# Reordering the hand-over from attention to the experts: expert sums ahead of the routers, two routers between the first pair's tiles

## The chip, the cores and the metric

One core of a Trainium2 chip runs the whole program. The metric is the device time of one execution in microseconds (us), as the median over several runs. TensorE is called PE, VectorE DVE, ScalarE ACT, GpSimd POOL and SyncE SP. Each engine works through its own queue of instructions in order; semaphores tie the queues together.

## The reference, cut to what matters

There are B = 4 batches of 512 tokens with D = 512 features. A cross-attention block of smoothed int8 products comes first, then a feed-forward block with 8 experts of which the two with the largest summed logits are used for all tokens:

```python
x = x + _L0_xattn_ref(_layernorm(x), fside_BxS2xS2_0, ctx_1024)

# _L0_ffn_ref(_layernorm(x), ...)
x = hidden_states.reshape(-1, d)                      # 2048 tokens x 512
router_logits = x @ gate_w.T                          # 2048 x 8
_, sel = jax.lax.top_k(router_logits.sum(axis=0), 2)  # two experts for all tokens
rw = jax.nn.softmax(router_logits[:, sel], axis=1)
w1s, b1s, w2s, b2s = w1[sel], b1[sel], w2[sel], b2[sel]
h = jax.nn.gelu(jnp.einsum('nd,kdf->knf', x, w1s) + b1s[:, None, :])
y = jnp.einsum('knf,kfd->knd', h, w2s) + b2s[:, None, :]
out = jnp.einsum('nk,knd->nd', rw, y)                 # added to x
```

## The kernel before

The first part (to about 131 us of the span) is the quantised attention block: four batches, two products each, with transposes on PE between them. Its PSUM is handed out as four "slots" of two banks; `SLOT_USES` lists by hand who uses each slot in which order, `fill` waits until the earlier uses of a slot are drained, and `drained` counts them.

The second part is the feed-forward block. The 16 "pairs" (2 experts x 8 strips of 256 hidden features) each multiply all 2048 tokens, in two halves (tp = 0, 1), with the strip's up-projection, apply GELU and multiply with the down-projection. The 15 later pairs use Strassen's scheme with seven products instead of eight; the first pair is computed plainly (`plain`, line 850) while the operands of Strassen's scheme are still being made. All products are fp32 in two parts: each operand is split into a rounded "hi" part (ACT casts) and a remainder "lo" part (subtraction on DVE or POOL), and hi*hi, hi*lo and lo*hi are accumulated. A plain tile is 12 products of 128x512.

The hand-over between the two parts is where the diff lies. For each batch b and feature half h:

- `normed2(b, h)` on PE (line 656) transposes the normalised tokens into slot use `y.b.h`.
- ACT copies them to SBUF (`keep_full`, line 961, which also sums over tokens, or `keep_summed`, line 968, where DVE's `token_sums`, line 1334, makes the sum), then rounds them (`keep_hi`, line 973). DVE makes the remainder (`keep_lo`, line 1291), the "split".
- `router(b)` on PE (line 667): 8 products that give the logits of all 512 tokens of a batch; ACT's `keep_logits` (line 982) copies them to SBUF. `logit_columns(b)` (line 685) transposes them into bank 3, and DVE's `pick_logits` (lines 1361 to 1368) takes the two chosen experts' columns; POOL raises e to their difference (`pow`, line 523), DVE makes the softmax weights (`token_weights`, lines 1519 to 1523). Every later `outputs_of` (line 1541), which adds a weighted product of the down-projection to the residual and frees the PSUM bank for PE, needs these weights.
- `token_total` (line 1342) adds the token sums, `expert_sums` on PE (line 677) multiplies them with the gate's weights, `choose_experts` on DVE (lines 1346 to 1349) finds the two experts; SP waits for that, reads the numbers and loads the first strip of weights, `raw1` (line 285) and `raw2` (line 289). ACT's `first_weights` (line 985) rounds the four blocks of `raw1`, DVE's (line 1381) makes the remainders; then the first plain tile can start.
- POOL's `inv_std(b, 2)` (lines 340, 341: a `pow` and a product) gives the second normalisation's factors; batch 3 is normalised half by ACT (line 895) and half by DVE (`normalise_last`, line 1323).

The order in each queue is written out by hand. Before, on PE: `normed2(3, 1)`, `router(1)`, `expert_sums`, `router(0)`, `router(2)`, `router(3)`, then in the first pair tiles 0 and 1, the logit columns, tiles 2 and 3, the four `down` groups (line 805: 48 products for two token groups of 512 and two feature strips), then the second half likewise. On DVE the `keep_lo` of all batches stand ahead of the remainders of the first weights. The second half of `down` starts a bank only after `outputs_of` has freed it (`y_free`).

## Time and profile before

| | |
|---|---|
| median of 3 runs | 820.45 us (818.23 to 821.61) |
| span of the profiled execution | 818.7 us |
| PE busy | 771.5 us (94%) |
| DVE / ACT / POOL busy | 477.7 / 354.6 / 449.7 us |
| mean granted clock of PE | 0.979 of full speed |
| chain that ended last | PE 83%, POOL 8%, DVE 3% |

Of the profiled execution only the span, from the first to the last instruction, is shown; it lies 1.75 us under the median of the runs and inside their spread. The views are read as follows. A timeline line gives start, duration (of a merged run of instructions, from the first's start to the last's end), engine, line of the kernel, operation, destination and source, shape, and how many; square brackets give the idle time of the engine ahead of it and who ended it. PE's ends are modelled, so successive products overlap in the record: their pitch is read from starts. The granted clock is a share of 2.4 GHz, so 0.50 is the level of 1.2 GHz.

### The profile page before, as it was taken

To read this page: it belongs to the slowest core of one execution; us is meant where nothing else is said; L and a number is where in the kernel's file an instruction comes from. 1 tells how busy PE (TensorE), PEld (TensorE's weight loads), DVE (VectorE), ACT (ScalarE), POOL (GpSimd) and SP (SyncE) were. 2 spreads that over 40 slices of the span, in tenths; PEclk is the share of its full clock that TensorE was granted. 3 is DMA by queue.
4 is the path that set the end of the run, shared out by engine and by line. 5 is a ranking of instruction groups with operands and counts; after the bars stand their busy time and mean duration, and the time that the engine had idled before them with its cause. 6 is when DMAs were issued, how large, how long until landed. Compare 5 with 4: busy or idle time off the path is not lost.

```text
span 818.7 us, 11342 instructions
## 1 busy us (share of the span) xinstructions
PE 771.5 (94%) x3570; PEld 624.1 (76%) x3577; DVE 477.7 (58%) x669; ACT 354.6 (43%) x660; POOL 449.7 (55%) x497
## 2 busy tenths in 40 slices
PE   5688666999999999999999999999999999999998
PEld 4666455688788888888888888888888888888886
DVE  5999759797754545454545454545454545454545
ACT  3967588743442434343424343434343434242422
POOL 1789997157564646464646464646464646464622
PEclk9899968999999999999999999999999999999999
DMA  9400000301010101010101010101010101010022
GB/s 344 173 2 1 1 0 2 129 1 51 1 52 1 51 0 49 3 50 2 48 4 51 1 45 6 42 9 44 7 41 11 36 15 36 15 32 19 0 103 104
DMA packets 19077, 32.34 MB, mean 39 GB/s; under 512 B 872, under 2 KB 11240, under 8 KB 18160
## 3 DMA queue, kind: packets, MB, share of 16 engines
q1 hardware_dynamic: 18896, 31.98, 11.1%
q8 instruction: 12, 0.20, 0.1%
q10 hardware_dynamic: 160, 0.08, 0.0%
q14 instruction: 9, 0.07, 0.0%
HBM read 27.87 MB, written 4.19 MB: 39 GB/s over the span
## 4 chain that ended last, share of the span: by engine, by line
PE 83%; POOL 8%; DVE 3%; issue 2%; ACT 2%; DMA 1%; ACTq 0%; POOLq 0%; DVEq 0%
PE slot L805 42%; PE slot L792 34%; PE slot L850 3%; POOL wv L366 2%; POOL xf L383 1%; PE slot L667 1%; POOL wv L372 1%; POOL cv L366 1%; PE slot L585 1%; DVE rmax L1226 1%; DMA b_rows<-in_L_ffn_b 1%; POOL rstd L340 1%; POOL h_lo L476 1%; DVE stats L1217 1%; DVE peak_x L1226 1%
## 5 line engine op out<-in xcount | busy, mean ns | idle before, releaser
L792 PE MATMUL slot<-xo,a_hi 128*128 128x512 f32 x840 | 259.1, 390 | 0.0
L1541 DVE SCALAR_TENSOR_TENSOR res<-slot,rw,res 128x512 f32<-128x512 f32 x256 | 178.5, 750 | 130.3 <-PE slot L805 130.2
L1570 DVE TENSOR_TENSOR e<-slot,e 128x512 f32<-128x512 f32 x150 | 103.8, 692 | 173.4 <-PE slot L792 173.3
L805 PE MATMUL slot<-w_hi,h_hi 128*128 128x512 f32 x512 | 201.3, 393 | 0.4 <-POOL h_lo L476 0.4
L805 PE MATMUL slot<-w_lo,h_hi 128*128 128x512 f32 x512 | 199.6, 390 | 0.0
L805 PE MATMUL slot<-w_hi,h_lo 128*128 128x512 f32 x512 | 199.4, 390 | 0.0
L792 PEld LDWEIGHTS slot<-xo,a_hi 128*128 128x128 f32 x840 | 157.4, 188 | 33.3 <-DVE e L1570 0.2
L476 POOL TENSOR_TENSOR h_lo<-e,h_hi 128x512 fp32r<-128x512 f32 x96 | 138.1, 1451 | 55.0 <-ACT e L1104 54.0
L792 PE MATMUL slot<-xo,a_lo 128*128 128x512 f32 x420 | 163.7, 390 | 0.0
L805 PEld LDWEIGHTS slot<-w_hi,h_hi 128*128 128x128 f32 x512 | 96.1, 188 | 25.1 <-POOL h_lo L476 5.6
L476 POOL TENSOR_TENSOR h_lo<-hid,h_hi 128x512 fp32r<-128x512 f32 x32 | 44.1, 1378 | 124.7 <-ACT hid L1104 124.7
L805 PEld LDWEIGHTS slot<-w_hi,h_lo 128*128 128x128 f32 x512 | 96.2, 188 | 20.1
L805 PEld LDWEIGHTS slot<-w_lo,h_hi 128*128 128x128 f32 x512 | 96.2, 188 | 19.3
L792 PEld LDWEIGHTS slot<-xo,a_lo 128*128 128x128 f32 x420 | 78.9, 188 | 16.5
L1103 ACT ACTIVATE h_hi<-e,b_now 128x512 fp32r<-128x512 f32 x90 | 64.9, 721 | 58.0 <-DVE e L1570 57.6
L1142 ACT COPY e<-slot 128x512 f32<-128x512 f32 x30 | 17.6, 587 | 164.5 <-PE slot L792 164.5
L490 POOL TENSOR_TENSOR a_lo<-raw,a_hi 128x256 fp32r<-128x256 f32 x45 | 34.3, 761 | 95.9 <-ACT a_hi L988 95.9
L991 ACT CAST w_hi<-raw 128x512 fp32r<-128x512 f32 x32 | 19.8, 622 | 109.8 <-PE slot L805 109.8
L495 POOL TENSOR_TENSOR w_lo<-raw,w_hi 128x512 fp32r<-128x512 f32 x30 | 38.7, 1289 | 50.4 <-ACT w_hi L991 50.4
L1104 ACT ACTIVATE e<-e,b_now 128x512 f32<-128x512 f32 x90 | 63.8, 709 | 0.0
L1103 ACT ACTIVATE h_hi<-slot,b_now 128x512 fp32r<-128x512 f32 x38 | 26.2, 689 | 66.5 <-PE slot L792 56.6
L490 POOL TENSOR_TENSOR a_lo<-ssum,a_hi 128x256 fp32r<-128x256 f32 x60 | 43.7, 739 | 0.0
(145 smaller groups left out, 814.5 us busy)
## 6 DMA issues: line engine op xcount, KB each, us to landing
raw<-in_L_ffn_w SPq DMA_DIRECT2D x32, 512.0 KB, 3.4
res<-in_x SPq DMA_DIRECT2D x4, 1024.0 KB, 11.9
wv<-in_fside_BxS2xS SPq DMA_DIRECT2D x4, 1024.0 KB, 12.8
out_x<-res SPq DMA_DIRECT2D x3, 1024.0 KB, 3.9
cv<-in_ctx SPq DMA_DIRECT2D x4, 512.0 KB, 13.1
out_x<-res SPq DMA_DIRECT2D x4, 256.0 KB, 2.7
b_row<-in_L_ffn_b SPq DMA_DIRECT2D x2, 256.0 KB, 4.6
b_rows<-in_L_ffn_b ACTq DMA_DIRECT2D x1, 64.0 KB, 6.0
```

The costliest lines, as they stand in the source:

```text
L366: g.tensor_tensor(w[:, j, :], w[:, j, :], rows[b][:, 0:n], ALU.mult).then_inc(wmul_ready[b], 1)
L476: g.tensor_tensor(h_lo[:, i, :], hid[i][:, :], h_hi[:, i, :].bitcast(F32), ALU.subtract).then_inc(h_ready, 1)
L490: g.tensor_tensor(a_lo[:, i, :, :], A_OF[i], a_hi[:, i, :, :].bitcast(F32), ALU.subtract).then_inc(a_ops_ready, 1)
L495: g.tensor_tensor(w2_lo[:, f, :], raw2[:, f, :], w2_hi[:, f, :].bitcast(F32), ALU.subtract).then_inc(w2_ready, 1)
L792: last = t.matmul(dst, a[:, i, k, :], xo[tp][:, v, k, :], start=(start and n == 0), stop=(n == 3 * H - 1), skip_group_check=True)
L805: last = t.matmul(y_bank[j][:, :], a[:, i, j * P:(j + 1) * P], v[:, f, :], start=(start and n == 0), stop=(not start and n == 2), skip_gro ...
L850: last = t.matmul(TILE_BANK[n], a[:, 2 * f + h, k, :], xo[q][:, v, k, :], start=(m == 0), stop=(m == 3 * KD - 1))
L991: s.copy(w2_hi[:, f, :], raw2[:, f, :]).then_inc(w2_hi_ready, 1)
L1103: s.activation(h_hi[:, i, :], src, ACT.Gelu_apprx_tanh, bias=bias).then_inc(hid_ready, 1)
L1104: s.activation(hid[i][:, :], src, ACT.Gelu_apprx_tanh, bias=bias).then_inc(hid_ready, 1)
L1541: v.scalar_tensor_tensor(out=r, in0=y_bank[j][:, :], scalar=rw[:, ds(p, 1), n:n + 1].rearrange("p a b -> p (a b)"), in1=r, op0=ALU.mult, o ...
L1570: v.tensor_tensor(dst[:, :], src, other[:, :], ALU.add).then_inc(comb_ready, 1)
```

## The change

- PE: `expert_sums` moves ahead of all routers; of these only `router(1)` and `router(0)` stay ahead of the first plain tile, `router(2)` goes behind tile 0 and `router(3)` behind tile 1; the logit columns go from behind tile 1 to behind tile 2. 28 transposes of the identity into a spare bank (`keep_clock`) are added ahead of `normed2(2, 0)` and 12 ahead of `normed2(3, 0)`.
- PE: in a plain tile the products go hi*hi, hi*lo, lo*hi by groups of two; the wait ahead of them is for the rounded weights alone, and the wait for the weights' remainders stands ahead of lo*hi.
- DVE: `normalise_last` is first behind `moments(3, 2)`; `keep_lo(0, 0)` and `keep_lo(0, 1)` go behind `choose_experts`; then come `pick_experts`, `pick_bias`, `first_weights`, and only then the splits of batches 2 and 3, then the first down weights. `last_operands(0)` and `fourth_operand(0)` go ahead of `pick_logits`.
- ACT: `keep_summed(3, 1)` moves ahead of the roundings of batch 2, `keep_logits(1)` between those of batches 2 and 3, `keep_logits(0)` behind the first weights, `keep_logits(2)` and the first down weights behind the GELUs of tile 0, `keep_logits(3)` behind those of tile 1.
- SP: the first load of `raw1` is split in two of half its size, each with a semaphore of its own.
- The slots of the four routers' results are dealt out anew. POOL's order is unchanged.

```diff
@@ SLOT_USES
-             "r.0 "),
+             "r.1 "),
...
-             "a.2 s2.0 p2.0.1 y.3.1 r.3 "),
+             "a.2 s2.0 p2.0.1 y.3.1 "),
...
-             "s2.2 p2.1.1 p2.2.1 wq2.3 p2.3.0 y.1.1 y.2.0 r.1 "),
+             "s2.2 p2.1.1 p2.2.1 wq2.3 p2.3.0 y.1.1 y.2.0 r.0 "),
...
-             "p1.2.0 r2.0 wq1.3.0 r2.1 xq2.0 a.3 wq2.1 wq2.2 p2.2.0 s2.3 p2.3.1 y.1.0 y.2.1 e r.2 "),
+             "p1.2.0 r2.0 wq1.3.0 r2.1 xq2.0 a.3 wq2.1 wq2.2 p2.2.0 s2.3 p2.3.1 y.1.0 y.2.1 e r.2 r.3 "),
@@ SP
-            load_w1(0)
+            first = w1_v[ds(expert[0], 1), 0].rearrange("e p k f -> (e p) k f")
+            sp.dma_start(raw1[:, 0:H, :], first[:, 0:H, :]).then_inc(raw1_top, 16)
+            sp.dma_start(raw1[:, H:KD, :], first[:, H:KD, :]).then_inc(raw1_load, 16)
@@ PE
+            def keep_clock(n):
+                i, uses = place("y.3.1")
+                pe.wait_ge(drained[i], uses)
+                for _ in range(n):
+                    t.transpose(slot[i][:, 1, 0:P], ident[:, :], ident[:, :])
...
             normed2(1, 1)
+            keep_clock(28)
             normed2(2, 0)
             normed2(2, 1)
+            keep_clock(12)
             normed2(3, 0)
             normed2(3, 1)
+            expert_sums()
             router(1)
-            expert_sums()
             router(0)
-            router(2)
-            router(3)
@@ plain
-                        pe.wait_ge(a_ops_ready, 2 * f + h + 1)
+                        pe.wait_ge(a_hi_ready, 2 * f + h + 1)
                     pe.wait_ge(lo_ready[b], h + 1)
                     hi, lo = HI_AT[s][h], LO_AT[s][h]
-                    for k in range(H):
-                        for a, v in ((a_hi, hi), (a_hi, lo), (a_lo, hi)):
+                    for a, v in ((a_hi, hi), (a_hi, lo), (a_lo, hi)):
+                        if q == 0 and a is a_lo:
+                            pe.wait_ge(a_ops_ready, 2 * f + h + 1)
+                        for k in range(H):
@@ PE, first pair
+            up_tile(0, 0)
+            router(2)
+            up_tile(0, 1)
+            router(3)
+            up_tile(0, 2)
+            logit_columns(0)
+            logit_columns(1)
+            logit_columns(2)
+            logit_columns(3)
+            up_tile(0, 3)
+            first_downs(0)
@@ ACT
+            keep_summed(3, 1)
             keep_hi(2, 0)
             keep_hi(2, 1)
-            keep_summed(3, 1)
+            keep_logits(1)
             keep_hi(3, 0)
             keep_hi(3, 1)
-            keep_logits(0)
-            keep_logits(1)
             first_weights(0, 2)
             first_weights(2, 4)
             s.activation(gelu_warm[:, :], half[:, 0:1], ACT.Gelu_apprx_tanh)
-            keep_logits(2)
-            keep_logits(3)
-            first_down_weights()
+            keep_logits(0)
...
+            first_bias()
+            gelu_tile(0, 0)
+            keep_logits(2)
+            first_down_weights()
+            gelu_tile(0, 1)
+            keep_logits(3)
+            gelu_tile(0, 2)
+            gelu_tile(0, 3)
@@ DVE
             moments(3, 2)
-            keep_lo(0, 0)
+            normalise_last()
             keep_lo(1, 0)
-            normalise_last()
             token_sums(2)
-            keep_lo(1, 1)
             token_sums(3)
             token_total()
+            keep_lo(1, 1)
+            choose_experts()
+            keep_lo(0, 0)
             keep_lo(0, 1)
-            choose_experts()
+            pick_experts()
+            pick_bias()
+            first_weights(0, 2)
+            first_weights(2, 4)
             keep_lo(2, 0)
             keep_lo(2, 1)
             keep_lo(3, 0)
             keep_lo(3, 1)
-            first_weights(0, 2)
-            first_weights(2, 4)
-            pick_experts()
-            pick_bias()
-            first_down_weights()
-            pick_logits()
...
+            first_down_weights()
+            last_operands(0)
+            fourth_operand(0)
+            pick_logits()
+            token_weights()
+            outputs_of(0, 0, 0)
```

## Rows read from the trace of the kernel before

**Rows 1.** The page of the profile: the span.
```profile
span 818.7 us, 11342 instructions
```

**Rows 2.** The chain that ended last, in order of time: start, length, piece.
```profile
153.71 5.47 PE slot L850 x24
...
165.97 10.88 PE slot L805 x48
```

**Rows 3.** PE's timeline through the hand-over.
```profile
122.37 1.04 PE L616 MATMUL slot<-ident,cv 128*128 128x128 f32 x8
...
134.49 0.41 PE L656 MATMUL slot<-ident,xf 128*128 128x128 f32 x2 [3.44 <-POOL xf L396]
...
139.89 3.87 PE L656 MATMUL slot<-ident,xf 128*128 128x128 f32 x16 [0.81 <-ACT xf L895]
...
146.38 0.95 PE L677 MATMUL slot<-gwt_full,tok_total 128*128 128x8 f32 x8
147.19 6.52 PE L667 MATMUL slot<-xo,gwt 128*16 128x512 f32 x24
...
159.11 1.17 PE L685 MATMUL slot<-ident,logits 16*128 16x16 f32 x16
...
165.81 0.39 PE L805 MATMUL slot<-w_hi,h_hi 128*128 128x512 f32 x1
```

**Rows 4.** Busy time by stretch: length; PE, PEld, DVE, ACT, POOL; clock; DMA share, GB/s.
```profile
83.00:84.00 1.00, 0.00 (x0) 0.06 (x2) 0.82 (x1) 0.72 (x1) 0.95 (x2) 1.00 0.00 0
...
135.00:136.00 1.00, 0.55 (x3) 0.30 (x4) 0.93 (x8) 1.00 (x3) 1.00 (x3) 0.72 0.00 0
...
145.00:146.00 1.00, 1.00 (x5) 0.31 (x3) 0.87 (x3) 1.00 (x2) 0.00 (x0) 0.66 0.00 0
```

**Rows 5.** DVE's timeline through the hand-over.
```profile
135.98 2.86 DVE L1291 TENSOR_TENSOR xo<-xf,xo 128x1024 fp32r<-128x1024 f32 x2
...
143.79 1.23 DVE L1334 TENSOR_REDUCE tok_sum<-slot 128x2 f32<-128x1024 f32 x1 [1.59 <-PE slot L656]
145.15 0.17 DVE L1342 TENSOR_REDUCE tok_total<-tok_sum 128x4 f32<-128x16 f32 x1
...
147.38 0.17 DVE L1346 COPY sum_row<-slot 128x8 f32<-128x8 f32 x1 [0.93 <-PE slot L677]
...
147.94 4.61 DVE L1291 TENSOR_TENSOR xo<-xf,xo 128x1024 fp32r<-128x1024 f32 x4
152.60 1.43 DVE L1381 TENSOR_TENSOR a_lo<-raw,a_hi 128x256 fp32r<-128x256 f32 x4
...
155.84 0.29 DVE L1375 TENSOR_REDUCE b_col<-picked 128x16 f32<-128x128 f32 x1
...
162.44 0.18 DVE L1366 TENSOR_TENSOR lsub<-lmin,lmax 128x16 f32<-128x16 f32 x1
...
166.60 1.24 DVE L1519 TENSOR_TENSOR lexp<-lpow,is_top 128x16 f32<-128x16 f32 x2
...
170.07 2.73 DVE L1541 SCALAR_TENSOR_TENSOR res<-slot,rw,res 128x512 f32<-128x512 f32 x4
```

**Rows 6.** ACT's timeline: rounding of batch 2, and of the first weights.
```profile
144.13 2.01 ACT L973 CAST xo<-xf 128x1024 fp32r<-128x1024 f32 x2
...
152.16 1.33 ACT L985 CAST a_hi<-raw 128x256 fp32r<-128x256 f32 x4 [1.87 <-DMA raw<-in_L_ffn_w]
```

**Rows 7.** POOL's timeline: the powers, and the remainders of the hidden tiles.
```profile
34.58 1.03 POOL L340 TENSOR_TENSOR rstd<-var_e,neg_half 128x4 f32<-128x4 f32 x1
...
136.60 1.97 POOL L340 TENSOR_TENSOR rstd<-var_e,neg_half 128x4 f32<-128x4 f32 x1
...
162.69 2.90 POOL L523 TENSOR_TENSOR lpow<-euler,lsub 128x16 f32<-128x16 f32 x1 [0.84 <-DVE lsub L1366]
165.56 3.43 POOL L476 TENSOR_TENSOR h_lo<-e,h_hi 128x512 fp32r<-128x512 f32 x2
```

**Rows 8.** SP's timeline: the issue of the first weights.
```profile
148.99 0.39 SPq L285 DMA_DIRECT2D raw<-in_L_ffn_w  x1
```

More of the change, by code:

```diff
@@ L881, in _, with first_downs @@
-            first_pair()
+                if n == 3:
+                    pe.wait_ge(hid_ready, 8 + 8 * tp + 2)
+                if tp == 0 and n == 0:
+                    pe.wait_ge(drained[0], ALL_DRAINED[0])
+                if tp == 0 and n == 2:
+                    pe.wait_ge(drained[1], ALL_DRAINED[1])
+                plain(tp, n)
+            def first_downs(tp):
+                if tp == 0:
+                    pe.wait_ge(w2_ready, 2)
+                    pe.wait_ge(drained[2], ALL_DRAINED[2])
+                    pe.wait_ge(drained[3], ALL_DRAINED[3])
+                down(0, tp, 0, 0, 0, True)
+                down(0, tp, 0, 1, 1, False)
+                last = down(0, tp, 1, 2, 1, True)
+                if tp == 1:
+                    last.then_inc(w2_free, 1)
+                down(0, tp, 1, 3, 0, False)
@@ L882, in _ @@
+            up_tile(0, 0)
[9 more added lines that the diff above has]
+            first_downs(0)
+            for n in range(4):
+                up_tile(1, n)
+            first_downs(1)
+            pe.wait_ge(hid_ready, 8 + 16)
             pair(1, True, False)
@@ L1173, in pair @@
                         down_hi(0)
-            first_pair()
+            first_bias()
[6 more added lines that the diff above has]
+            gelu_tile(0, 3)
+            operand_hi(0, (T2H, T2L), 4)
+            operand_hi(0, (T3H, T3L), 4)
+            operand_hi(0, (T1H, T1L), 4)
+            operand_hi(0, (T4H, T4L), 4)
+            for n in range(4):
+                gelu_tile(1, n)
+            later_weights()
             pair(1, True, False)
@@ L1596, in pair @@
                         operand_lo(1, 3)
-            first_pair()
+            first_down_weights()
[4 more added lines that the diff above has]
+            outputs_of(0, 0, 0)
+            middle_operands(0, 3)
+            middle_operands(0, 4)
+            outputs_of(0, 0, 1)
+            operand_lo(0, 0)
+            operand_lo(0, 1)
+            operand_lo(0, 2)
+            operand_lo(0, 3)
+            last_operands(1)
+            fourth_operand(1)
+            dve.wait_ge(b2_load, 16 * TOPK)
+            bias_rows(0)
+            outputs(0, 1)
             pair(1, True, False)
```

91 lines of the change are left out of this document (28 added, 63 removed).

## The prediction

> **What bounds the kernel now.** I read the page first: a span of 818.7 us [rows 1]. The chain that ended last, in order of time, is then PE alone from the first plain tile on [rows 2]: 24 products of line 850 are followed by 48 of line 805 without a gap, and so on to the end, so whatever comes ahead of that stretch or opens a gap in it is added to the total one for one, and work of other engines inside it costs nothing while PE isn't kept waiting. Therefore the timelines of the hand-over decide, PE's first [rows 3]: idle for 3.44 us up to 134.49; 16 transposes of batch 3 from 139.89 in 3.87 us, where 8 elsewhere take 1.04; then router 1, the expert sums at 146.38, three routers from 147.19, the first plain tile (it begins behind them, 153.55), the logit columns at 159.11, the first down product at 165.81. The stretches say why batch 3's transposes are slow [rows 4]: the granted clock fell from 2.4 to 1.2 GHz inside 135 to 136, after PE's idle time, and came back inside 145 to 146. DVE, ACT, POOL and SP then show what the first tile waits for [rows 5 to 8]. The point that I compare is the start of the first down product, 165.81 before: all of PE's work ahead of it is the same set in both kernels apart from `keep_clock`, and everything behind it is the same.
>
> **Prices.** A product of 128x512 at full clock has a pitch of 5.47/24 = 0.228 us [rows 2], so a plain tile is 2.73, a router without waits 8 x 0.228 = 1.82, the four down groups 10.88, two of them 5.44. A split on DVE is 1.15 (four in 4.61 [rows 5]), four weight remainders 1.43, `pick_experts` with `pick_bias` 156.13 - 154.03 = 2.1 [rows 5].
>
> **Step 1, up to batch 3's transposes.** 28 transposes at 1.04/8 = 0.13 each at most are 3.6 us; from the end of `normed2(1, 1)` (131.0) they fill the idle 3.44 us and end at 134.3 to 134.7, so they cost at most 0.2 us of a wait that is followed by another wait for POOL. The 12 take 1.4 and end at about 139.4. The clock should stay at 2.4 GHz: in the rows PE is only slowed after such a gap. On DVE the two splits that began at 135.98 leave the time in which POOL computes the last power. That power took 1.97 us beside them and 1.03 otherwise [rows 7], and ACT's and DVE's normalisation of batch 3 hang on it. I take the gain of 0.95: its factors are ready at 137.9 instead of 138.9. PE then transposes from about 139.3 (behind the 12) with 16 x 0.12, and ends at 141.3 instead of 143.76. What the row shows is a power stretched by 0.94 us when DVE's subtractions of two SBUF operands ran beside it. The Trainium skill, "SBUF — State Buffer", section "Who interferes with whom", says that a DVE instruction with two SBUF inputs contends with a GpSimd instruction that reads SBUF, the later one being blocked. By that rule the gain is real; without it the power would stay at 1.97 and the step would be 1 us poorer. The trace agrees with it here.
>
> **Step 2, the choice of experts.** Before: last token sum 143.79 (waiting for PE), total at 145.15, expert sums at 146.38 behind router 1, result read at 147.38, index found at 148.02 [rows 3, 5]. After: `normalise_last`, one split and `token_sums(2)` end at 141.3, `token_sums(3)` 1.2 later, the total at 142.9; PE is free and starts at once, 143.15, the copy at 144.15, the index at 144.8. So 3.2 us earlier, 148.0 to 144.8. SP issued 0.97 after the index [rows 8]; now 145.8. The rounding of the weights began 3.17 after the issue [rows 6], 148.9 for the whole; the first half should be there at about 148.2 (half of 512 KB moves in 0.7 us at the rate of that load, 330 GB/s). ACT is the later one: four roundings at 1.0 [rows 6] from 143.6, with `keep_logits(1)` between them waiting for router 1 (146.0), end at 148.5. First rounded block at 148.9.
>
> **Step 3, PE to the first down product.** Router 1 144.05 to 145.9; router 0 waits for its splits, which now stand behind the choice, and ends at 148.15; PE idles to 148.95. Tile 0 starts there, 4.6 us earlier than 153.55; its remainders are made from 149.35 on and don't hold it. But routers 2 and 3, 3.64 us, now lie behind. Router 2 also waits: DVE goes from 144.8 through two splits (2.3), picking (2.1 and gaps), remainders (1.43, from 149.35) and two splits (2.3) to 153.15, so router 2 ends at 154.1 where PE alone would allow 153.5: 0.55 lost. Then tile 1 156.85, router 3 158.65 (its slot is free once ACT has copied router 2's at 154.7), tile 2 161.4, columns 162.55 (1.15 by [rows 3]), tile 3, first down product at 165.3. Sum: -4.6 + 3.64 + 0.55 = -0.4; by the clock times -0.5. The earlier weights are spent on the routers moved behind them.
>
> **Step 4, the tokens' weights.** Before, the columns were done at 160.3, DVE's difference at 162.62, POOL's power to 165.6, the weights at 170.03, the first output freed its bank at 170.8, and PE's third down group, 5.44 behind the first, wanted it at 171.25: only 0.45 us of slack [rows 3, 5, 7]. After, the columns are 2.3 us later (162.55) though the down products start 0.5 earlier. Picking takes 2.3: difference at 164.9. The power, at 16 columns, is 2.9 by its row. Since it is 1.03 at 4 columns alone, it grows with the columns, and I don't expect it to be shorter with DVE idle: 167.8 (bounds: 1.03, were it all contention, and 2.9). DVE has `last_operands` and `fourth_operand` behind it now, so it starts at once, where it started 1.0 after the power before. Its small operations took 3.4 us there, next to two remainders on POOL (3.43 for two) [rows 5, 7]. The GELUs of tile 2 have been done since 162.7 and those of tile 3 at 166.6, and both remainders stand queued on POOL behind the power, so the same meeting takes place: I take 3.6, with a floor of 1.4 if DVE gets in first (the sum of these operations at their shortest, an estimate). Weights at 171.4, first output done at 172.2 (0.75). PE wants it at 165.3 + 5.44 = 170.75: a stall of 1.4, between 0 and 1.6. By the same section of the Trainium skill the one that comes later waits for the whole instruction, and POOL and DVE are released by the same event. The rule alone leaves either order open, which is my floor and my ceiling.
>
> **Step 5, behind it.** What DVE does in the first pair moves back by 1.4 as PE does: middle operands to 176.7, outputs to 179.5, remainders 184, last operands 189.7, bias 193.1. PE wants the second half's first bank at 177.6 + 10.92 + 5.44 = 194.0, and gets it at 193.8. So nothing is added, up to 0.5 if one of them is stretched. The new semaphore waits of the tiles are met long before.
>
> **Sum.** -0.5 + 1.4 = +0.9 us on the profiled execution, 819.6. The runs' median is 1.75 above the span, so I forecast 820.45 + 0.9 = 821.3. The measurement tells about 0.5%, 4.1 us, from no change.
>
> **Rivals.**
> 1. The weights' chain doesn't hold PE up: DVE's small operations get in ahead of POOL's remainders. Against it stand the 3.4 us of the same operations before. Then only -0.5 is left: 820.0, with somewhat more if a split or the picking ends sooner. Chance 0.27.
> 2. Slower: the clock. In the new order PE idles from 141.3 to 143.1 for the token sums, then 0.3 and 0.8 us within 147 to 149. If the clock drops to 1.2 GHz as it did in 135 to 136, each product of 128x512 costs twice, and the rows' low stretch lasted 10 us under broken work. Five microseconds of low clock on work that isn't waiting cost 2.5, ten cost 5, added to +0.9: 823.8 to 826.2. For it: the fall at 135 followed idle time. Against: PE had nothing to do for all of 83 to 84 at a clock of 1.00 [rows 4]. [...] Chance 0.12. The Trainium skill, "TensorE: Matmul & The Clock Gate", section "What's actually happening", says that the clock depends on how busy the array has been recently and that throttled is the default; it names no price for gaps like these.
> 3. The change doesn't do what it says: `keep_clock` doesn't keep the clock, or POOL's power stays long. Batch 3's transposes then end 1 to 2 us later and the whole chain with them: +1.9 to +2.9, 822.3 to 823.4. Chance 0.15.
> 4. The front gains more than I have worked out, because PE's order has more freedom: the most is what PE's own work allows. From 139.3 it has 1.9 + 0.95 + 4 x 1.82 + 4 x 2.73 + 1.15 = 22.2 us, so the down products can't start before 161.5, 4.3 us earlier. That needs all waits of steps 2 to 4 to vanish. A gain of 1 to 3 us: chance 0.05.
>
> The forecast itself has 0.41. **Range**: 818.0 to 824.5; it takes in rivals 1 and 3 and the milder end of 2, and the 1.7 us by which the runs scatter. Faster by over 0.5% would need rival 4 whole: 0.03. Slower by over 0.5% is the hard end of rival 2, or 2 with 3: 0.07. Within: 0.90.
>
> **What would show it.** Clock 1.00 from 131 to the end; the power of batch 3 at 1.03; the index at 144.8; first tile at 149, with a gap of under 1 us ahead of it; router 2 waiting for DVE's split; first down product at 165.3; then a gap of 1.4 in PE at about 170.8, ended by DVE's line 1541 behind the weights. If the gap is missing, step 4 is wrong; if the clock shows 0.50 behind 141, rival 2 it is; if the first down product comes before 164 or after 167, steps 2 and 3 are.

## The result and the profile after

| | before | after |
|---|---|---|
| median | 819.89 us (818.23 to 821.80, 7 runs) | 822.36 us (821.68 to 823.69, 7 runs) |
| span of the profiled execution | 818.7 us | 820.3 us |
| mean granted clock of PE | 0.979 | 0.985 |
| ratio to before, with its 95% interval | | 1.0039 [1.0024, 1.0053] |

The forecast was 821.3 us, within 818.0 to 824.5, with a change of under half a per cent as the likeliest outcome. That is what came: the change makes the kernel a little slower. By the two medians the loss is 2.5 us (a quotient of 1.0030); the ratio of 1.0039 on record, with its interval, puts it at 2.0 to 4.3 us. Between the two profiled executions it is 1.6 us; I had +0.9.

The page of the profile after, its span and its first part (busy time, share, instructions):

```profile
span 820.3 us, 11435 instructions
PE 773.2 (94%) x3617; PEld 624.6 (76%) x3617; DVE 479.4 (58%) x669; ACT 354.7 (43%) x660; POOL 448.7 (55%) x497
```

PE is busy 1.7 us longer than before: the 40 transposes of `keep_clock` add 4.7 (3.22 and 1.47), and at the full clock batch 3's transposes and router 1 take less. PE's timeline of after, through the hand-over, to be read against [rows 3]:

```profile
130.58 3.22 PE L666 MATMUL slot<-ident 128*128 128x128 f32 x28
...
138.86 2.10 PE L659 MATMUL slot<-ident,xf 128*128 128x128 f32 x16
142.58 1.06 PE L686 MATMUL slot<-gwt_full,tok_total 128*128 128x8 f32 x8 [1.62 <-DVE tok_total L1377]
143.49 4.23 PE L676 MATMUL slot<-xo,gwt 128*16 128x512 f32 x16
148.57 1.17 PE L862 MATMUL slot<-xo,a_hi 128*128 128x512 f32 x4 [0.85 <-ACT a_hi L1008]
...
152.12 2.16 PE L676 MATMUL slot<-xo,gwt 128*16 128x512 f32 x8 [0.57 <-DVE xo L1326]
...
161.52 1.16 PE L695 MATMUL slot<-ident,logits 16*128 16x16 f32 x16
...
165.49 0.39 PE L815 MATMUL slot<-w_hi,h_hi 128*128 128x512 f32 x1
...
170.71 0.39 PE L815 MATMUL slot<-w_hi,h_lo 128*128 128x512 f32 x1
172.57 0.47 PE L815 MATMUL slot<-w_hi,h_hi 128*128 128x512 f32 x1 [1.48 <-DVE res L1574]
```

Everything that the change says is there: the 16 transposes of batch 3 take 2.10 us instead of 3.87, the expert sums start at 142.58 instead of 146.38, the first plain tile at 148.57 instead of 153.55. And yet the first down product starts at 165.49 instead of 165.81. Behind it is what before didn't have: PE stands still at the third down group, for 172.57 - 170.71 - 0.23 = 1.63 us, until DVE has written the first output. From the first down product's start to the end nothing else is new: the only further gap in the groups of this line is 0.4 us for a POOL remainder, as in before.

DVE's timeline of after, against [rows 5]:

```profile
142.36 0.17 DVE L1377 TENSOR_REDUCE tok_total<-tok_sum 128x4 f32<-128x16 f32 x1
...
144.16 0.16 DVE L1384 FIND_INDEX8 top_i<-top_v,sum_row 128x8 uint32<-128x8 f32 x1
...
150.76 5.73 DVE L1326 TENSOR_TENSOR xo<-xf,xo 128x1024 fp32r<-128x1024 f32 x4
...
164.91 0.17 DVE L1401 TENSOR_TENSOR lsub<-lmin,lmax 128x16 f32<-128x16 f32 x1
...
168.17 1.27 DVE L1552 TENSOR_TENSOR lexp<-lpow,is_top 128x16 f32<-128x16 f32 x2 [2.91 <-POOL lpow L524]
169.36 1.27 DVE L1553 TENSOR_SCALAR lden<-lpow 128x16 f32<-128x16 f32 x1
170.66 0.25 DVE L1554 RECIPROCAL lrec<-lden 128x16 f32<-128x16 f32 x1
170.95 0.69 DVE L1556 TENSOR_TENSOR rw<-lexp,lrec 128x128 f32<-128x128 f32 x2
```

POOL's of after, against [rows 7]; then ACT's (the rounding of the first block and of the other three) against [rows 6], and SP's issue against [rows 8]:

```profile
136.32 1.00 POOL L343 TENSOR_TENSOR rstd<-var_e,neg_half 128x4 f32<-128x4 f32 x1
...
165.17 2.90 POOL L524 TENSOR_TENSOR lpow<-euler,lsub 128x16 f32<-128x16 f32 x1 [5.19 <-DVE lsub L1401]
168.03 2.56 POOL L479 TENSOR_TENSOR h_lo<-e,h_hi 128x512 fp32r<-128x512 f32 x2
```

```profile
147.92 0.40 ACT L1008 CAST a_hi<-raw 128x256 fp32r<-128x256 f32 x1
149.29 1.02 ACT L1008 CAST a_hi<-raw 128x256 fp32r<-128x256 f32 x3 [0.97 <-DMA raw<-in_L_ffn_w]
```

```profile
145.29 0.39 SPq L294 DMA_DIRECT2D raw<-in_L_ffn_w  x1
```

The end of the chain that ended last, before and then after (start, length, piece): it is 1.52 us later.

```profile
803.73 9.02 PE slot L805 x39
```

```profile
805.25 9.03 PE slot L815 x39
```

### The profile page after: what moved, and what is told of

Its sections match the earlier page's. It is cut to its first block, busy times and chain, and to the rows that moved or that the text cites. A ratio compares the mean times of both kernels' runs of the same rounds, so it can differ in the third digit from the quotient of the medians.

```text
span 820.3 us, 11435 instructions
## 1 busy us (share of the span) xinstructions
PE 773.2 (94%) x3617; PEld 624.6 (76%) x3617; DVE 479.4 (58%) x669; ACT 354.7 (43%) x660; POOL 448.7 (55%) x497
## 4 chain that ended last, share of the span: by engine, by line
PE 80%; POOL 8%; DVE 5%; issue 3%; ACT 2%; DMA 1%; SPq 0%; ACTq 0%; POOLq 0%; DVEq 0%
PE slot L815 41%; PE slot L802 34%; PE slot L862 2%; POOL wv L369 2%; POOL xf L386 1%; POOL wv L375 1%; POOL cv L369 1%; PE slot L588 1%; DVE rmax L1261 1%; DMA b_rows<-in_L_ffn_b 1%; POOL h_lo L479 1%; DVE stats L1252 1%; DVE peak_x L1261 1%; PE slot L638 1%; ACT xf L918 1%
## 5 line engine op out<-in xcount | busy, mean ns | idle before, releaser
L1163 ACT COPY e<-slot 128x512 f32<-128x512 f32 x30 | 17.6, 587 | 164.4 <-PE slot L802 164.4
```

What stands on the lines that cost most here:

```text
L1163: s.copy(e1[:, :], x_bank).then_inc(e1_ready, 1)
```

## The experiments

Executions differ ahead of the part in question: the start of POOL's last normalising (`xf<-res,rstd,nmr`), which I call N, lies at 133.0 to 134.6 us in kernels whose code is the same up to there but for the first transposes of `keep_clock`. So I compare distances: "front" is the start of the first down product minus N, "rest" is the span minus N. The ratios are those on record, with their intervals; they are not exactly the quotients of the medians shown (the two differ by up to 0.0009, most in after), so a difference of less than 0.1% between kernels is not told by either. Each profile is one execution.

| kernel | N | normalising / power on POOL | front | rest | median (runs) | ratio |
|---|---|---|---|---|---|---|
| before | 133.58 | 3.05 / 1.97 | 32.23 | 685.1 | 819.89 (7) | |
| after | 133.30 | 3.05 / 1.00 | 32.19 | 687.0 | 822.36 (7) | 1.0039 [1.0024, 1.0053] |
| e1_clock_alone | 134.43 | 4.05 / 1.96 | 30.90 | 684.1 | 820.51 (12) | 1.0003 [0.9991, 1.0016] |
| e2_no_clock | 133.81 | 3.05 / 1.00 | 32.71 | 687.3 | 823.27 (5) | 1.0041 [1.0028, 1.0054] |
| e3_hid2_first | 133.82 | 3.01 / 1.01 | 33.41 | 688.4 | 823.1 (5) | 1.0035 [1.0022, 1.0048] |
| e4_front_alone | 133.25 | 3.05 / 1.00 | 31.05 | 684.2 | 819.5 (11) | 0.9997 [0.9988, 1.0005] |
| e5_one_load | 134.47 | 3.01 / 1.01 | 32.15 | 687.0 | 822.69 (12) | 1.0032 [1.0021, 1.0043] |
| e6_pool_waits | 134.63 | 3.05 / 1.00 | 32.29 | 685.3 | 821.09 (12) | 1.0013 [1.0003, 1.0024] |
| e7_both | 133.60 | 3.01 / 1.01 | 32.07 | 685.2 | 820.69 (12) | 1.0011 [1.0, 1.0022] |
| e8_pool_split | 133.74 | 3.05 / 1.00 | 29.94 | 683.1 | 818.8 (12) | 0.9983 [0.9972, 0.9995] |
| e9_before_again | 133.72 | 4.09 / 1.97 | 33.31 | 686.6 | 820.05 (10) | 0.9997 [0.9983, 1.0011] |
| e10_router_in_gap | 134.53 | 3.05 / 1.01 | 31.24 | 684.3 | 819.5 (12) | 0.999 [0.9978, 1.0002] |
| e11_before_third | 134.44 | 3.05 / 1.97 | 29.99 | 682.9 | 819.17 (1) | |
| e12_split_no_clock | 133.00 | 3.05 / 1.00 | 32.24 | 685.1 | 820.6 (12) | 1.0008 [0.9997, 1.0019] |

Rest less front is what the kernel takes from the first down product to its end. It is 654.6 to 655.0 us in the four kernels whose profile has the stall at the third down group (after, e2, e3, e5), and 652.9 to 653.3 in the ten others: 1.8 us apart in the mean, with nothing between.

### e1_clock_alone: before, with only `keep_clock`

```diff
             normed2(1, 1)
+            keep_clock(28)
             normed2(2, 0)
             normed2(2, 1)
+            keep_clock(12)
             normed2(3, 0)
```

> The kernel before with the 28 and 12 transposes of keep_clock and nothing else. Theory (batch 3's transposes at 1.2 GHz delay the expert sums, and only DVE's splits stand between these and tile 0): the last transpose ends at about 142.2 instead of 143.8, router 1 fits into PE's wait for the token sums, the index is found at 145.7 instead of 148.0, the four splits follow, tile 0 starts near 151.3 instead of 153.55, and since the routers stay ahead of tile 0 and the columns behind tile 1, no stall appears in the down products: 2.2 us faster than before, ratio 0.997. Rival (the clock is worth nothing, since PE waits for DVE and ACT anyway): 1.000, with 40 useless transposes.

The clock stayed at 1.00 through the whole stretch. The front came 1.33 us nearer to N than in before's profile, less than the 2 us that I gave the clock, because POOL's last normalising took 4.05 us instead of 3.05: DVE's splits had caught it. By medians the gain isn't there at all: 1.0003. The profile and the medians contradict each other here, and this is where the study turned to before itself (e9, e11).

### e2_no_clock: after, without `keep_clock`

```diff
             normed2(1, 1)
-            keep_clock(28)
             normed2(2, 0)
             normed2(2, 1)
-            keep_clock(12)
             normed2(3, 0)
```

> The changed kernel without keep_clock. Theory: the clock falls at about 135, batch 3's transposes end 1.8 later and everything up to the first down product shifts with them, the stall for the tokens' weights stays at 1.6: 1.9 us slower than the changed kernel, 3.4 slower than before, ratio to before 1.004 to 1.006. Rival (the 40 transposes themselves cost time in the changed kernel): equal to the changed kernel or faster.

The clock was 0.50 from 136 to 139.4 and was back before PE had to wait for the token sums; the ratio is after's (1.0041 against 1.0039). So in this order `keep_clock` buys nothing that these runs can tell, since PE has to wait for DVE's token sums anyway. The stall is of the same size, and it has the same releaser:

```profile
173.60 0.47 PE L813 MATMUL slot<-w_hi,h_hi 128*128 128x512 f32 x1 [1.48 <-DVE res L1572]
```

### e3_hid2_first: after, with one of POOL's two remainders ahead of the power

The step in question is Step 4: are the tokens' weights late because POOL's remainders run beside them?

```diff
             hid_lo(0, 0, 1)
-            token_power()
             hid_lo(0, 0, 2)
+            token_power()
             hid_lo(0, 0, 3)
```

> The changed kernel with POOL's remainder of tile 2 ahead of the power. Theory (the stall ahead of the third down group is the tokens' weights, and 2.4 of their 3.5 us is DVE blocked by two remainders on POOL): the remainder is made at about 163 while POOL idles, only tile 3's is left to meet DVE, the weights come 1.2 earlier and the stall falls from 1.6 to about 0.4: 1.2 us faster than the changed kernel, ratio to before about 1.001. Rival (the DVE operations are slow by themselves or wait for something else): the stall stays at 1.6 and the time is that of the changed kernel.

The stall stayed: 174.40 - 172.44 - 0.23 = 1.73 us. POOL's queue behind the power is the reason; its timeline:

```profile
169.77 1.29 POOL L479 TENSOR_TENSOR h_lo<-e,h_hi 128x512 fp32r<-128x512 f32 x1
171.01 0.76 POOL L484 TENSOR_TENSOR ssum<-raw 128x256 f32<-128x256 f32 x1
171.85 0.73 POOL L486 TENSOR_TENSOR ssum<-ssum,raw 128x256 f32<-128x256 f32 x1
```

and DVE's, beside it:

```profile
169.91 1.27 DVE L1552 TENSOR_TENSOR lexp<-lpow,is_top 128x16 f32<-128x16 f32 x2 [2.91 <-POOL lpow L524]
171.09 0.71 DVE L1553 TENSOR_SCALAR lden<-lpow 128x16 f32<-128x16 f32 x1
171.84 0.25 DVE L1554 RECIPROCAL lrec<-lden 128x16 f32<-128x16 f32 x1
172.13 1.34 DVE L1556 TENSOR_TENSOR rw<-lexp,lrec 128x128 f32<-128x128 f32 x2
```

`lexp` ends where the remainder does, `lden` where the first sum of weights does, `rw` only behind the second and third. I had moved one of POOL's instructions away, and the next in its queue took its place; the weights still took 3.56 us. Moving work about in a queue that never runs dry takes no collision away. This run's front is also 1.2 us longer than after's: the second half of the split load landed 5.3 us behind the first issue here, instead of 4.0.

### e6_pool_waits: POOL held back until the weights are made

```diff
             hid_lo(0, 0, 1)
-            token_power()
             hid_lo(0, 0, 2)
+            token_power()
+            pool.wait_ge(rw_made, 1)
             hid_lo(0, 0, 3)
...
             token_weights()
+            dve.sem_inc(rw_made, 1)
             outputs_of(0, 0, 0)
```

> The changed kernel with POOL's remainder of tile 2 ahead of the power and POOL kept idle from the power until DVE has the tokens' weights. Theory (these DVE operations are slow only beside POOL's, whichever they are): they take 1.4 instead of 3.5 us, the first output's bank is free before PE wants it, the stall of 1.5 at the third down group is gone: 1.5 us faster than the changed kernel, ratio to before about 1.002. Rival (the operations are slow by themselves): the stall stays.

DVE's timeline and then POOL's:

```profile
169.60 0.26 DVE L1554 TENSOR_TENSOR lexp<-lpow,is_top 128x16 f32<-128x16 f32 x2 [2.91 <-POOL lpow L525]
169.78 0.17 DVE L1555 TENSOR_SCALAR lden<-lpow 128x16 f32<-128x16 f32 x1
169.98 0.25 DVE L1556 RECIPROCAL lrec<-lden 128x16 f32<-128x16 f32 x1
170.27 0.50 DVE L1558 TENSOR_TENSOR rw<-lexp,lrec 128x128 f32<-128x128 f32 x2
```

```profile
170.90 1.30 POOL L480 TENSOR_TENSOR h_lo<-e,h_hi 128x512 fp32r<-128x512 f32 x1 [1.40 <-DVEq L1622]
```

The same operations take 170.77 - 169.60 = 1.17 us instead of 3.47, PE has no gap at the third down group any more, and the rest falls by 1.7 us while the front is after's. From e3, which has the stall, this kernel differs by the wait alone. This shows what Step 4 said: the stall is POOL's remainders beside DVE's small operations. Its price is 1.8 us by the profiles (from the first down product on), 1.3 by the medians of after and e6, and 2.0 by those of e5 and e7 below, which were measured together, 12 times each, and differ only in this: the larger part of the loss. The power itself stays at 2.90 with nothing beside it.

The rule that I had weighed, in the Trainium skill, "SBUF — State Buffer", section "Who interferes with whom", is that the order of issue decides who blocks. The traces agree where the starts lie clearly apart: in after and in e3 POOL's remainder began 0.14 us ahead of DVE's first operation, and DVE's 0.17 us operations lasted as long as POOL's. It works the other way round too: later in e6, two of POOL's sums of weights of 0.73 us took 1.72 beside DVE's operands. Where the starts are about 0.1 us apart or less they don't tell who waits: in e9 and e1 below, POOL's piece began 0.08 and 0.10 us ahead of DVE's split and was yet the one that waited.

### e5_one_load and e7_both: the first strip loaded in one piece

e5 is after with the diff below; e7 is e6 with it.

```diff
-            sp.dma_start(raw1[:, 0:H, :], first[:, 0:H, :]).then_inc(raw1_top, 16)
-            sp.dma_start(raw1[:, H:KD, :], first[:, H:KD, :]).then_inc(raw1_load, 16)
+            load_w1(0)
...
                     if i == 0:
-                        act.wait_ge(raw1_top, 16)
-                    if i == 1:
                         act.wait_ge(raw1_load, 16)
```

> The changed kernel with the first weights in one load instead of two halves. Theory (the second half lands late: ACT got it 4.0, 4.5 and 5.3 us after the first issue in three profiles of kernels with two halves, the whole load 3.2 and 3.5 after the issue in two with one): the rounding of all four blocks begins 3.2 to 3.5 after the issue, DVE's splits of batch 2 start 0.5 to 1.3 earlier than with the halves, and the down products with them: 0.5 to 1.3 us faster than the changed kernel, ratio to before 1.002 to 1.003. Rival (the late second half is hidden behind PE's own work, or the first half is worth as much): the time of the changed kernel, 1.004.

> Both at once: one load, and POOL idle for the tokens' weights. Theory: the two add up, 2.0 to 2.8 us faster than the changed kernel, which is within 0.5 us of before, ratio 0.9995 to 1.001: what is left of the change is worth nothing, because the moved routers take back what the earlier choice gives. Rival (another part costs too): over 1.002.

In one piece the load is there 3.38 us behind its issue in e5 and 3.46 in e7 (3.17 in before). In two pieces, the first half is used at most 2.63 us behind the first issue (145.29 to 147.92 in after), and the second only 4.00 (after), 4.11 (e6), 4.54 (e2) or 5.30 (e3) behind it. The halves are issued 0.57 apart. Against 3.4 for the whole, that is nearly all of the delay in after and e6, but half or less of it in e2 and e3; why the second half is later still there isn't shown. The first tile then starts earlier, but the remainders of the last weights later, and with them the splits that router 2 waits for: the front is 32.15 and 32.07 against 32.19 and 32.29. The ratios (1.0032 against 1.0039, 1.0011 against 1.0013) don't tell them apart. Splitting the load brings nothing here that these runs can tell.

### e4_front_alone: only the part ahead of the choice of experts

Before with `keep_clock`, the expert sums first, DVE's `normalise_last` first and its splits behind the choice, ACT's `keep_summed(3, 1)` early. The routers and the logit columns stay where before has them.

```diff
+            keep_clock(28)
...
+            keep_clock(12)
...
-            router(1)
             expert_sums()
+            router(1)
...
-            keep_lo(0, 0)
-            keep_lo(1, 0)
             normalise_last()
+            keep_lo(1, 0)
             token_sums(2)
-            keep_lo(1, 1)
             token_sums(3)
             token_total()
-            keep_lo(0, 1)
+            keep_lo(1, 1)
             choose_experts()
+            keep_lo(0, 0)
+            keep_lo(0, 1)
```

> The changed kernel's front (keep_clock, normalise_last first, expert sums ahead of router 1, splits of batch 0 behind the choice) with the routers, columns and splits of batches 2 and 3 where they stood before. Theory: index at 144.5, the six splits end at 151.2, PE runs four routers and starts tile 0 at 152.0, where before started at 153.5; no stall for the tokens' weights, since the columns are behind tile 1: 1.3 us faster than before, 0.9985, and 2.8 faster than the changed kernel, so that the moved routers cost all that and more. Rival (moving the routers helps, and the stall would be there in any case once the front is earlier): slower than before or equal to it.

The front is 31.05, 1.14 nearer than after's, with the same choice of experts (index at N + 10.86 in both). So what after has beyond e4 (two routers behind the tiles, the splits behind the weights, the split load, the order of the products) costs 1.1 us ahead of the first down product, and its late columns cost the stall. Against before's medians e4 gains nothing that can be told (0.9997). Its DVE row says why:

```profile
144.19 6.88 DVE L1299 TENSOR_TENSOR xo<-xf,xo 128x1024 fp32r<-128x1024 f32 x6
```

Six splits behind the choice instead of four (4.61 in [rows 5]). Before makes two of them while POOL computes its power, which costs POOL 0.97 us; here the power is 1.00, but DVE owes 2.3 us of splits later, and the weights, which ACT had begun to round at 148.70, wait for DVE until 150.99.

### e8_pool_split: e4, with one of these splits on POOL

POOL is idle from the last power on. It makes the first split of batch 0, once DVE is through the first of batch 1, so beside token sums that read PSUM and not two operands from SBUF.

```diff
             inv_std(3, 2)
+            pool.wait_ge(hi_ready[0], 1)
+            pool.wait_ge(lo_ready[1], 1)
+            g.tensor_tensor(whole(0, LO_AT[0][0]), part(0, FULL_AT[0][0]),
+                            whole(0, HI_AT[0][0]).bitcast(F32), ALU.subtract).then_inc(lo_ready[0], 1)
...
             choose_experts()
-            keep_lo(0, 0)
+            dve.wait_ge(lo_ready[0], 1)
             keep_lo(0, 1)
```

> e4 with batch 0's first split on POOL, which waits for batch 1's first split and so runs beside the two token sums. Theory (in e4 tile 0 waits for DVE's chain of splits, which runs without a break from the sums to the weights' remainders): one split less on it, tile 0 starts 1.15 earlier than in e4, 1.2 us faster than e4, ratio to before 0.998. Rival (POOL's split takes more from DVE than it gives, or PE's routers are the bound by themselves): that of e4, 0.9997, or worse.

POOL's row, DVE's and PE's:

```profile
140.36 2.36 POOL L473 TENSOR_TENSOR xo<-xf,xo 128x1024 fp32r<-128x1024 f32 x1 [2.32 <-DVE xo L1303]
```

```profile
144.68 5.75 DVE L1303 TENSOR_TENSOR xo<-xf,xo 128x1024 fp32r<-128x1024 f32 x5
```

```profile
143.94 7.65 PE L677 MATMUL slot<-xo,gwt 128*16 128x512 f32 x32
...
163.68 0.39 PE L817 MATMUL slot<-w_hi,h_hi 128*128 128x512 f32 x1
```

The front is 29.94, 1.1 less than e4's, one split of DVE; the four routers run almost without a gap (7.65 us, of which 7.28 are their own work), and the last of them still waits for DVE's last split. With 0.9983 [0.9972, 0.9995] it is faster than both kernels: 0.17% below before, and by the two ratios to before (0.9983 and 1.0039) 0.56% below after (by the medians 0.13% and 0.43%). How much of the gain on before is the order and how much the clock, the next section bears on.

### e9_before_again and e11_before_third: before, profiled again

No edit. The question is how far one profiled execution of before stands for it.

> The kernel before, unchanged, for a second profile. In the profiles so far the span behind the start of POOL's normalisation of batch 2 is 685.1 (before), 687.0 (changed kernel), 685.2 (one load and POOL waiting), while the medians of these differ by 2.5 and 0.9. Theory (what the traces show behind that point is the change's whole cost, and the rest is the time ahead of it, where the code is the same and executions scatter by over 1 us): the second profile of before has 685.1 again behind that point, and its time ahead of it is not 133.6 but nearer to 132.8; ratio 1.000. Rival (the first profile of before was unusual behind that point): it shows 684.4 or less there.

> The kernel before once more, for a third profile. Over 91 executions of this kernel so far the span goes with the mean granted clock: 817.2 to 817.5 us at 0.982 and above, 819.3 and more at 0.979 and below; the two profiles so far are of the second kind (0.979 with 818.7, 0.976 with 820.3), with PE at 1.2 GHz for some 10 us of the hand-over. Theory (the kernel before is two-sided: how long the clock stays low behind PE's idle time, and whether POOL's last normalising is caught behind DVE's split, differ from execution to execution): an execution with a clock of 0.982 or more shows a low stretch of 3.4 to 7 us there, a first down product 31 us behind the start of POOL's normalisation of batch 2 instead of 32.2 or 33.3, and a span near 817.5. Rival (the difference lies elsewhere): 32.2 whatever the clock.

e9, POOL's timeline and then DVE's:

```profile
133.72 4.09 POOL L396 TENSOR_SCALAR xf<-res,rstd,nmr 128x512 f32<-128x512 f32 x4
137.78 1.97 POOL L340 TENSOR_TENSOR rstd<-var_e,neg_half 128x4 f32<-128x4 f32 x1
```

```profile
136.03 2.85 DVE L1291 TENSOR_TENSOR xo<-xf,xo 128x1024 fp32r<-128x1024 f32 x2
```

e11, the stretches (as in [rows 4]), and PE's row:

```profile
136.00:137.00 1.00, 0.67 (x3) 0.43 (x4) 0.93 (x8) 1.00 (x2) 1.00 (x2) 0.80 0.00 0
...
139.00:140.00 1.00, 0.94 (x5) 0.54 (x3) 0.91 (x2) 0.21 (x1) 0.68 (x2) 0.50 0.00 0
140.00:141.00 1.00, 0.25 (x2) 0.21 (x2) 1.00 (x3) 1.00 (x2) 0.00 (x0) 1.00 0.03 8
```

```profile
164.43 0.39 PE L805 MATMUL slot<-w_hi,h_hi 128*128 128x512 f32 x1
```

The same program has fronts of 32.23, 33.31 and 29.99. Two things differ. The normalising is four pieces of 0.77 us, and in before's order the splits begin at almost the same moment as the fourth of them: 0.15 us behind it in before's profile and 0.12 in e11, where the piece took 0.8 and the split 1.7 instead of 1.2, and 0.08 in e9 and 0.10 in e1, where the piece took 1.8 to 1.9 and the split 1.2. A few hundredths of a microsecond go with who waits: half a microsecond for DVE, or one for POOL, on which batch 3 hangs. And the low clock lasted 10 us in before's profile (135.4 to 145.7) and in e9 (136.0 to 146.2), but under 4 in e11 (136.6 to 140), where batch 3's transposes and router 1 found the full clock again. With e1 the four fronts are consistent with a sum: e9 less before is 1.1 and e1 less e11 is 0.9, the caught normalising; before less e11 is 2.2 and e9 less e1 is 2.4, the long stretch of low clock. Over the 95 timed executions of before that were made beside e1 to e12, the mean clock and the span go together: 48 with a clock of 0.982 or more have a median span of 817.4 us, 30 with 0.979 or less one of 819.8, and 17 between them 818.2. That the long stretch is what sets the lower clock of those 30 is worked out from three profiles, not seen in each. By its clock of 0.979 the profile that I predicted from is of the kind of the 30, though its span of 818.7 is among their shortest.

This explains only a part of e1. If the long stretch belongs to a third of before's executions, `keep_clock` has little to remove in the others, and hardly moves a median. But all 12 timed executions of e1 have a clock of 0.982 or more, and still their median span is 818.6 us, 1.2 above that of the 48 of before with such a clock. e4 has `keep_clock` too, but no split beside the normalising, and has 817.6. The caught normalising, 1 us in e1's profile, would account for the difference; whether e1's other executions have it isn't shown. By the same measure e8, with 816.9, is 0.5 us ahead of the 48, and its front of 29.94 is e11's: about half of what it gains on before's median span (817.9) may be the long stretch that it doesn't have.

### e12_split_no_clock: e8 without `keep_clock`

The diff is e2's, on e8.

> e8, the fastest so far, without keep_clock. Theory (a shorter low stretch costs nothing while PE waits for the token sums anyway, as in e2, a longer one up to 2 us): 0.3 to 1 us slower than e8, ratio to before 0.9985 to 0.9995. Rival (the clock is worth nothing behind the new order): 0.9983.

A stretch of e12, its expert sums and its routers, and last the expert sums of e2:

```profile
144.00:145.00 1.00, 1.00 (x5) 0.37 (x5) 0.91 (x6) 1.00 (x2) 0.00 (x0) 0.52 0.00 0
```

```profile
143.09 1.06 PE L687 MATMUL slot<-gwt_full,tok_total 128*128 128x8 f32 x8 [1.62 <-DVE tok_total L1352]
144.01 9.13 PE L677 MATMUL slot<-xo,gwt 128*16 128x512 f32 x32
```

```profile
143.09 1.06 PE L686 MATMUL slot<-gwt_full,tok_total 128*128 128x8 f32 x8 [1.62 <-DVE tok_total L1375]
```

The clock was low from 133.8 to 140.6, came back, and was low a second time from 144.0 to 147.4, behind the 1.6 us in which PE waits for the token sums. The routers took 9.13 us instead of 7.65, and the front is 32.24 instead of 29.94. Of these 2.3 us the first low stretch has 0.8 (the index comes at N + 11.67 instead of 10.86, since PE's slow transposes hold up the token sums) and the second 1.5. By the ratios it is 1.0008 against 0.9983, 2 us, and 1.8 by the medians, where I had expected 0.3 to 1. It is my rival 2, in an order like after's but without `keep_clock`: with the idle time filled ahead of it, the same wait for the token sums left the clock at 1.00 (after, e4 to e8). But the missing transposes alone don't bring it about: e2 lacks them as well, has the same wait of 1.62 us, and kept 1.00 behind it. Its first low stretch was 3.4 us long and e12's 6.8; the cause of the difference isn't shown.

### e10_router_in_gap: can that wait be used?

e8, with router 1 ahead of the expert sums, both of batch 1's splits ahead of the token sums, and after's order of products in a plain tile.

```diff
-            pool.wait_ge(lo_ready[1], 1)
+            pool.wait_ge(lo_ready[1], 2)
...
             normed2(3, 1)
-            expert_sums()
             router(1)
+            expert_sums()
...
             keep_lo(1, 0)
+            keep_lo(1, 1)
             token_sums(2)
             token_sums(3)
             token_total()
-            keep_lo(1, 1)
             choose_experts()
```

> e8 with batch 1's second split ahead of the token sums, router 1 ahead of the expert sums and the changed kernel's order of products in a plain tile (the wait for the weights' remainders only ahead of the last products). Theory (in e8 PE runs four routers without a break from 143.9 to 151.4 and idles 1.6 us ahead of the expert sums): router 1 moves into that idle time, the expert sums come 1.1 later, the other three routers end at 150.7 and tile 0 starts there on rounded weights that landed at about 150.4: 0.8 us faster than e8, ratio to before 0.9973. Rival (the later index delays the weights and DVE's splits by as much): that of e8, 0.9983, or worse.

DVE's row, PE's, and a stretch:

```profile
145.85 0.17 DVE L1360 COPY sum_row<-slot 128x8 f32<-128x8 f32 x1 [1.15 <-PE slot L687]
```

```profile
147.67 6.02 PE L677 MATMUL slot<-xo,gwt 128*16 128x512 f32 x20 [0.92 <-DVE xo L1305]
```

```profile
147.00:148.00 1.00, 0.33 (x1) 0.11 (x2) 1.00 (x2) 1.00 (x2) 0.00 (x0) 0.50 0.00 0
```

The router does run in PE's wait, and the wait moves to DVE: the split ahead of the token sums delays the total and the index by 0.9 us against N, DVE then idles 1.15 us for the expert sums, and batch 0's split is late for its router. PE now waits twice (0.72 us ahead of the expert sums, 0.92 ahead of router 0's second half), and behind the last of these the clock was low from 147.0 to 150.4 though `keep_clock` is in the kernel: 20 of the routers' products took 6.02 us where 4.6 would be their full rate. Little of that 1.4 reaches the first tile, because DVE's last split, which the last router needs, ends only at 152.16, 17.6 behind N, where e8's ends 16.7 behind. Router 3's last product began 0.92 behind the end of that split, where e8's began 0.53 behind: the low clock has 0.4 of the front, and without it the front would be about 30.8 (an estimate), still behind e8's 29.94. The ratio, 0.999 [0.9978, 1.0002], doesn't tell it from e8's 0.9983. The wait for the token sums is no free room as long as what fills it needs DVE first, and breaking it up put the clock at risk.

## Why the prediction was right or wrong, step by step

**Step 1** held. The transposes of batch 3 ended at 140.96 (141.3 forecast), the power took 1.00, and the clock was 1.00 from 130 on. That the power's stretch goes with DVE's splits is shown by the twelve other profiles: 1.00 or 1.01 in the nine kernels that have no split there, 1.96 or 1.97 in e1, e9 and e11, which have it.

**Step 2** held: total 142.36 (142.9), index 144.32 (144.8), issue 145.29 (145.8), all half a microsecond early. The first half of the weights landed by 147.9, the second at 149.3; I had no term for a late second half (and for the first I had divided wrongly: 256 KB at 330 GB/s are 0.8 us, not 0.7).

**Step 3** held on its sum, with a wrong part that another one hid. The first tile started at 148.57 (148.95), router 2 waited 0.57 (0.55), tile 1 started at 154.12 (154.1), the columns at 161.52 (161.4), the first down product at 165.49 (165.3). The splits of batches 2 and 3 took 5.73 us where I had 4.6, because the last of the four met POOL's first remainder and took 2.32; nobody waited for that one. What I got wrong is what the earlier tile was measured against. Of its 4.98 us, by the two profiles, 2.3 are not in an execution like e11, whose low stretch is short: its first tile starts at N + 17.65, after's at N + 15.27, 2.4 earlier. In return after has two routers (3.84 by their starts) and 0.72 ahead of router 2 between the tiles, so against e11 the order loses 2.2 us at the first down product. "The earlier weights are spent on the routers moved behind them" was the right sentence; against an execution like e11 they are overspent, and by the clock of the timed executions more than half of before's may be like it.

**Step 4** held and is the main loss: difference 164.91 (164.9), power 2.90 (2.9) and not the 1.03 of the other bound, weights 3.47 from 168.17 (3.6), stall 1.63 (1.4). The term was 0.2 short, since the power began only at 165.17, 0.26 behind the start of the difference. e6 shows the cause and the price, e3 that it can't be dodged by moving one remainder.

**Step 5** held: no new wait in the second half. Between the gap and the end after loses another 0.2 us (1.32 at the third down group, 1.52 at the last), which I haven't located.

**The sum.** Three terms of +0.2 each (the front, the stall, the part behind) make +0.9 into the 1.5 to 1.6 of the two profiles. The other 0.9 between that and the 2.5 of the medians isn't the change but the reference: before's profiled span is 818.7, its median execution's 819.89 - 1.9 = 818.0, where 1.9 is the median difference of time and span in before's runs. Here the conversion that I used was weak: I took the median of three runs for the profile's own time. It happened to be within 0.2 us of it (820.6), so the forecast time was only 1.1 off while the forecast difference was 1.6 off. That the time came so near is in part luck.

**The rivals.** Rival 1 (DVE gets in first) didn't occur by itself; e6 shows that it is worth 1.3 to 2.0 us. Rival 2 (the clock) didn't occur in after's profile, but it is real: e12 and e10 show it, behind waits of 1.6 and of 0.7 and 0.9 us. After, e2 and e8 have 1.6 without it, so the length of the wait alone doesn't tell. Its upper time was added up a little short: 820.45 + 0.9 + 5 is 826.35. Rival 3 is out for the clock and for the power. Rival 4 needed waits to vanish that e8 only partly removes: the best front found is 29.94, which an execution of before itself (e11) has too.

**Still open:** why N itself scatters between 133.0 and 134.6 for the same instructions, why the low clock lasts under 4 us in some executions and 10 in others, what keeps e1's executions 1.2 us above those of before with the same clock, and what of e10's fall at 147 belongs to its order and what to that one execution. No execution of before at the fast end (a span of 816.2 us) was profiled.

## What to carry to other kernels

Where two engines in a hand-over start on the same event, look at what each has queued next and not at what each does alone: one small chain behind a shared release cost 3.5 us instead of 1.2, and a wait on the busier engine took it away, where reordering its queue didn't. An instruction that fills another engine's idle time isn't free to move out of it: the split that lengthened POOL's power by a microsecond had saved DVE more. And before a difference of 1 or 2 us is worked out from one profile, set its span and its mean clock against those of the timed runs: by its clock, this profile belonged to a third of them.

## What the runs showed of the hardware

- After a gap of about 3.5 us on PE, in the broken work that follows it, the granted clock went to 1.2 GHz in all five profiles that have the gap (before, e2, e9, e11, e12), from 0.1 us ahead of its end to 1.4 behind it; it stayed there for 3.4 us in one execution of the same program and for 10 in two others. Forty fp32 transposes of an identity in the idle time (4.7 us of PE in rows, no one waiting) kept it at 2.4 GHz in all nine profiles that have them, up to the choice of experts; in eight it stayed so, and in e10 it fell at 147, behind two shorter waits. They were worth nothing that the runs can tell in after's order, where PE then waits anyway (e2), and 2 us in e8's (e12).
- DVE operations of 0.17 us lasted as long as the POOL subtraction or sum they met (up to 1.27); POOL's pieces of 0.73 lasted 1.72 where DVE had come first, and its last normalising 4.09 instead of 3.05.
- Two halves of a 512 KB load, issued 0.57 us apart, had their second half in use 4.00 to 5.30 us behind the first issue; the whole in one piece took 3.17 to 3.76 in the profiles where ACT was waiting for it.
- POOL's power takes 1.00 us for 4 columns and 2.90 for 16, with DVE idle beside both.
